# The experts layer computed by groups of four token tiles, with its weights held stationary

## The reference, cut to what matters

```python
shared = _silu_and_mul(x @ shared_gate_up_w.T) @ shared_down_w.T
shared = shared * jax.nn.sigmoid(x @ sgate_w.T)
routing_weights = jax.nn.softmax(x @ gate_w.T, axis=-1)
topk_w, topk_ids = jax.lax.top_k(routing_weights, 4)
for e in range(16):
    coef = jnp.sum(jnp.where(topk_ids == e, topk_w, 0.0), axis=-1)
    acc = acc + (_silu_and_mul(x @ w13[e].T) @ w2[e].T) * coef[:, None]
out = x_before_layernorm + shared + acc
```

## Time and profile before

| what | value |
|---|---|
| median of 3 runs | 3290.54 us (3288.26 to 3293.41) |
| the profiled execution's own time | 3290.39 us |
| its span in the trace | 3288.6 us |
| busy: PE, PEld, DVE, ACT, POOL | 2855.3, 1788.7, 1566.7, 1267.7, 1233.2 us |
| mean granted clock of PE, as a share of 2.4 GHz | 0.937 |
| experts stage, from its first instruction to the end of the span | 2635.61 to 3288.6 us |

### The profile page before, as it was taken

How to read it: one execution, slowest core, us unless ns; L and a number is a source line. 1 busy time by engine, 2 the same in 40 slices (tenths; PEclk the granted TensorE clock), 3 DMA queues, 4 the chain that set the end, 5 groups by cost and what they waited for, 6 DMA issues and landing times. The chain is left out here.

```text
span 3288.6 us, 50135 instructions
## 1 busy us (share of the span) xinstructions
PE 2855.3 (87%) x17687; PEld 1788.7 (54%) x17688; DVE 1566.7 (48%) x2714; ACT 1267.7 (39%) x2578; POOL 1233.2 (37%) x656
## 2 busy tenths in 40 slices
PE   6868444689999999999999999999978899999998
PEld 4646312554555555455545554555435567777776
DVE  3546587255445445544554455446427733333332
ACT  3437222134334433443344334334434423333332
POOL 0001000246567656765676576657650000000000
PEclk9879766779999999999999999999989999999999
DMA  1000300101111110110110111011012000000000
GB/s 42 0 15 0 125 0 0 59 26 41 37 40 36 40 36 25 51 40 25 36 51 33 33 36 51 25 40 36 31 39 115 1 1 0 0 0 0 0 0 26
DMA packets 26586, 98.13 MB, mean 30 GB/s; under 512 B 3808, under 2 KB 8544, under 8 KB 25120
## 3 DMA queue, kind: packets, MB, share of 16 engines
q1 hardware_dynamic: 24864, 94.15, 8.6%
q10 hardware_dynamic: 1664, 3.18, 0.3%
HBM read 55.71 MB, written 2.10 MB: 18 GB/s over the span
## 5 line engine op out<-in xcount | busy, mean ns | idle before, releaser
L742 POOL TENSOR_TENSOR cx_acc<-cx_acc,cx_prob 128x1024 f32<-128x1024 f32 (+1 forms) x352 | 834.5, 2371 | 509.1 <-ACT cx_prob L1022 501.6
L1022 ACT ACTIVATE cx_prob<-cx_st 128x512 f32<-128x512 f32 (+1 forms) x832 | 476.9, 596 | 595.4 <-PE cx_st L871 575.9
L1119 DVE TENSOR_REDUCE cx_mhalf<-cx_mx 128x1 f32<-128x804 f32 x512 | 486.3, 988 | 219.0 <-PE cx_mx L847 218.7
L882 PE MATMUL cx_av<-cx_prob,cx_kv 128*64 128x512 f32 (+1 forms) x1664 | 455.6, 626 | 0.0
L870 PE MATMUL cx_st<-cx_q,cx_k 128*128 128x512 f32 (+1 forms) x832 | 369.0, 444 | 49.7 <-ACT cx_prob L1022 49.0
L1585 PE MATMUL moe_gu<-moe_wgu,moe_xnT 128*128 128x352 f32 x1280 | 398.8, 463 | 0.0
L847 PE MATMUL cx_mx<-cx_kp,cx_q 128*128 128x402 f32 x1024 | 305.8, 382 | 61.9 <-DVE cx_mhalf L1119 58.6
L871 PE MATMUL cx_st<-cx_q,cx_k 128*128 128x512 f32 (+1 forms) x832 | 332.2, 399 | 0.0
L847 PEld LDWEIGHTS cx_mx<-cx_kp,cx_q 128*128 128x128 f32 x1024 | 176.0, 195 | 247.9 <-DVE cx_mhalf L1119 184.2
L1585 PEld LDWEIGHTS moe_gu<-moe_wgu,moe_xnT 128*128 128x128 f32 x1280 | 242.2, 191 | 124.7 <-issue 7.2
L1100 DVE TENSOR_TENSOR cx_turn<-cx_mx,cx_tab 128x384 f32<-128x384 f32 x256 | 130.9, 552 | 358.2 <-PE cx_mx L804 358.2
(11 more groups left out here) (210 smaller groups left out, 3648.3 us busy)
## 6 DMA issues: line engine op xcount, KB each, us to landing
cx_k<-cx_kp SPq DMA_DIRECT2D x32, 804.0 KB, 3.9
cx_ctx<-in_cx_ctxN SPq DMA_DIRECT2D x32, 416.0 KB, 3.3
cx_ctxr<-in_cx_ctxrN SPq DMA_DIRECT2D x32, 416.0 KB, 3.9
cx_k<-cx_kp SPq DMA_DIRECT2D x32, 402.0 KB, 5.1
moe_wgu<-in_moe_wgu SPq DMA_DIRECT2D x5, 1408.0 KB, 14.0
moe_wd<-in_moe_wd SPq DMA_DIRECT2D x4, 896.0 KB, 23.8
x_all<-in_x SPq DMA_DIRECT2D x1, 2048.0 KB, 3.9
cx_wq<-in_cx_wq SPq DMA_DIRECT2D x1, 2048.0 KB, 11.8
```

What stands on the lines that cost most here:

```text
L742: pool.tensor_tensor(acc[rows, :, :], sofar, prob[slot(kt)][rows, :, :], ALU.add).then_inc(s_acc, 1)
L882: last = pe.matmul(av[DCX * p:DCX * p + DCX, :], kv[e][0:nk(kt), kt, :], prob[slot(kt)][0:nk(kt), p, :], start=(kt == 0), stop=(kt == NKT ...
L1022: act.activation(prob[slot(kt)][rows, p, :], st[p][rows, :], ACT.Exp).then_inc(s_exp, 1)
L1119: dve.tensor_reduce(mhalf[:, i // 2, i % 2:i % 2 + 1], mx[i % 2][:, :, 0:KQ], AX.XY, ALU.max)\
```

## The change

The layer takes a group of four tiles (512 tokens) at a time, four groups in all, without a loop. The 3520 inner units are laid out as 28 chunks of 128 (the last padded with zeros), `moe_wgu` as `[P, 28, 2, DC, P]`. A chunk's weights are stationary and the 512 tokens of `xnT` move, so gate and up come out with inner units on partitions, ready for the down product: `turn` and its copies go. The coefficient is no longer one number per partition; a token's 17 coefficients (16 experts and the shared gate) are split in three bf16 parts (51 numbers), turned once per group by PE, and for each chunk a product with a 0/1 matrix `ownerb` of 51 rows spreads them to a PSUM tile `share` of 128 x 512. DVE multiplies silu with `share`, then with `up`. Each group is stored by its own DMA of 512 KB. The 0/1 matrix is one more load (f32, 51 x 3584) ahead of `a2`.

```diff
-    wgu = sb("moe_wgu", [P, NE, DC, 2 * FE])
+    wgu = sb("moe_wgu", [P, NFC, 2, DC, P])
+    owner = sb("moe_owner", [PARTS * CE, NFC, P])
-    pairs += [(wgu[:, 4 * i:4 * i + 4], a["moe_wgu"][:, 4 * i:4 * i + 4]) for i in range(NE // 4)]
+    pairs += [(wgu[:, 4 * i:4 * i + 4], a["moe_wgu"][:, 4 * i:4 * i + 4]) for i in range(NFC // 4)]
+    pairs += [(owner[:, :, :], a["moe_owner"])]
...
+    GATHER_AT = (3, 4)
+    NORM_AT = (6, 7)
+    TURN_AT = (9, 11)
+    KEEP_AT = (10, 12)
+    ROUTER_AT = 14
+    LOGITS_AT = 14
+    EXP_AT = 15
+    RANK_AT = 16
+    SPLIT_AT = 18
+    SPREAD_AT = 21
+    SPREAD_KEPT_AT = 22
...
+        @block.sync
+        def _(sp):
+            for g in range(NG):
+                sp.wait_ge(s_x, (g + 1) * GT)
+                sp.dma_start(out[g * GW:(g + 1) * GW, :].rearrange("(t p) d -> p t d", p=P),
+                             x_all[:, g * GT:(g + 1) * GT, :]).then_inc(s_out, 16)
...
+            def turn_coefficients(g):
+                pe.wait_ge(s_cf, g + 1)
+                for i in range(GT):
+                    last = pe.matmul(front[0:PARTS * CE, i * P:(i + 1) * P], parts[:, i, :, :], identb[:, :],
+                                     start=True, stop=True)
+            def gate_product(g, k):
+                if n >= 2:
+                    pe.wait_ge(s_silu, n - 1)
+                for c in range(DC):
+                    last = pe.matmul(gate[n % 2][:, :], wgu[:, k, 0, c, :], xnT[g % 2][:, c, :],
+                                     start=(c == 0), stop=(c == DC - 1))
+            def share_product(g, k):
+                if n == 0:
+                    pe.wait_ge(s_own, 1)
+                else:
+                    pe.wait_ge(s_gated, n)
+                pe.matmul(share[:, :], ownerb[:, k, :], coefT[g % 2][:, :], start=True, stop=True).then_inc(s_share, 1)
...
+            def down_product(g, k):
+                pe.wait_ge(s_hid, n + 1)
+                for i in range(GT):
+                    last = pe.matmul(acc[:, i, :], hidT[n % RING][:, i * P:(i + 1) * P], wd[:, k, :],
+                                     start=(k == 0 and i % 2 == 0), stop=(k == NFC - 1), skip_group_check=True)
...
+            turn_x(0, 0)
+            turn_x(0, 1)
+            router(0)
+            for g in range(NG):
+                for k in range(NFC):
+                    gate_product(g, k)
+                    if g == 0 and k == 0:
+                        up_product(g, k)
+                        turn_coefficients(0)
+                        share_product(g, k)
+                    else:
+                        share_product(g, k)
+                        up_product(g, k)
+                    if k >= LAG:
+                        down_product(g, k - LAG)
+                    elif g > 0:
+                        down_product(g - 1, NFC - LAG + k)
...
+            gather(0, 0)
+            gather(0, 1)
             normalise(0, 0)
-            logits(0, 0)
-            coefficients(0, 0)
-            rounds(dve, tile)
+            normalise(0, 1)
+            dve.tensor_copy(ownerb[:, :, :], owner[:, :, :]).then_inc(s_own, 1)
+            logits(0)
+            ranks(0)
+            split(0)
+            for g in range(NG):
+                for k in range(NFC):
+                    gated_product(g, k)
+                    hidden(g, k)
+                    if g > 0 and k == LAG - 1:
+                        update_x(g - 1)
...
-                sp.dma_start(out.rearrange("(t p) d -> p t d", p=P), x_all[:, :, :]).then_inc(s_out, 16)
```

More of the change, by code:

```diff
@@ new lines, in experts_weights, with experts_mlp @@
+    pairs += [(owner[:, :, :], a["moe_owner"])]
+    return (wgu, wd, wr, before, owner), pairs
+def experts_mlp(nc, sb, pb, sem, x_all, const, out, wgu, wd, wr, before, owner):
+    ident, identb = const["ident"], const["identb"]
+    stats = sb("moe_stats", [P, GT, 6])
+    mv = sb("moe_mv", [P, GT, 3])
+    rstd = sb("moe_rstd", [P, GT])
+    xn = sb("moe_xn", [P, GT, D])
+    xnT = [sb(f"moe_xnT{i}", [P, DC, GW]) for i in range(2)]
+    logit = sb("moe_logit", [P, GT, CE])
+    nmax = sb("moe_nmax", [P, GT])
+    rw = sb("moe_rw", [P, GT, CE])
+    rsum = sb("moe_rsum", [P, GT])
+    ahead = sb("moe_ahead", [P, GT, E, E])
+    equal = sb("moe_equal", [P, GT, E, E])
+    rank = sb("moe_rank", [P, GT, E])
+    coef = sb("moe_coef", [P, GT, CE])
+    rest = sb("moe_rest", [P, GT, CE])
+    parts = sb("moe_parts", [P, GT, PARTS, CE], BF16)
+    coefT = [sb(f"moe_coefT{i}", [PARTS * CE, GW], BF16) for i in range(2)]
+    ownerb = sb("moe_ownerb", [PARTS * CE, NFC, P], BF16)
+    RING = 3
+    silu = [sb(f"moe_silu{i}", [P, GW]) for i in range(RING)]
+    gated = [sb(f"moe_gated{i}", [P, GW]) for i in range(2)]
+    hidT = [sb(f"moe_hidT{i}", [P, GW]) for i in range(RING)]
+    gate = [pb(f"moe_gate{i}", [P, GW]) for i in range(2)]
+    up = [pb(f"moe_up{i}", [P, GW]) for i in range(2)]
+    share = pb("moe_share", [P, GW])
+    front = pb("moe_front", [P, GW])
+    acc = pb("moe_acc", [P, GT, D])
@@ L1531, in experts_mlp @@
     s_x = sem("moe_x_updated")
+    s_out = sem("moe_stored")
     s_dve = sem("moe_dve_step")
[L1533 to L1542, removed]
-    with nc.Block() as block:
+    LAG = 2
+    LAST = NG - 1
+    GATHER_AT = (3, 4)
+    NORM_AT = (6, 7)
+    TURN_AT = (9, 11)
+    KEEP_AT = (10, 12)
@@ L1546, in _ @@
         @block.gpsimd
         def _(pool):
[L1548 to L1558, removed]
+            for g in range(NG):
+                for half in range(2):
+                    tiles = slice(2 * half, 2 * half + 2)
+                    pool.wait_ge(s_var, 2 * g + half + 1)
+                    pool.tensor_tensor(rstd[:, tiles], mv[:, tiles, 1],
+                                       const["minus_half"][:, 0:1].broadcast_to([P, 2]), ALU.pow).then_inc(s_rstd, 1)
@@ new lines, in router @@
+            def router(g):
+                pe.wait_ge(s_xTc, 2 * g + 2)
+                for i in range(GT):
+                    for c in range(DC):
+                        last = pe.matmul(front[:, i * CE:(i + 1) * CE], xnT[g % 2][:, c, i * P:(i + 1) * P],
+                                         wr[:, c, :], start=(c == 0), stop=(c == DC - 1))
+                last.then_inc(s_rl, 1)
+            def turn_coefficients(g):
[3 more added lines that the diff above has]
+                                     start=True, stop=True)
+                last.then_inc(s_cT, 1)
@@ L1572, in router, with up_product @@
+            def up_product(g, k):
+                n = chunk(g, k)
+                if n >= 2:
+                    pe.wait_ge(s_hid, n - 1)
                 for c in range(DC):
-                    last = pe.matmul(front[:, 0:E + 1], xnT[g][:, c, :], wr[:, c, :],
+                    last = pe.matmul(up[n % 2][:, :], wgu[:, k, 1, c, :], xnT[g % 2][:, c, :],
                                      start=(c == 0), stop=(c == DC - 1))
[L1575 to L1626, removed]
@@ L1628, in _ @@
-            turn_x(0, 0)
-            router(0, 0)
-            rounds(pe, tile)
+                last.then_inc(s_up, 1)
+            def down_product(g, k):
+                n = chunk(g, k)
+                pe.wait_ge(s_hid, n + 1)
+                if k == 0 and g > 0:
+                    pe.wait_ge(s_x, g * GT)
+                for i in range(GT):
+                    last = pe.matmul(acc[:, i, :], hidT[n % RING][:, i * P:(i + 1) * P], wd[:, k, :],
+                                     start=(k == 0 and i % 2 == 0), stop=(k == NFC - 1), skip_group_check=True)
+                last.then_inc(s_down, 1)
@@ L1632, in _ @@
+            for k in range(NFC - LAG, NFC):
+                down_product(LAST, k)
         @block.scalar
         def _(act):
[L1634 to L1668, removed]
-            keep_xT(0, 0)
-            router_exp(0, 0)
@@ L1672, in _, with keep_xT, router_exp @@
-            rounds(act, tile)
+            def keep_xT(g, half):
+                act.wait_ge(s_xT, 2 * g + half + 1)
+                if g > 1:
+                    act.wait_ge(s_up, chunk(g - 2, NFC))
+                for i in range(2):
+                    at = (2 * half + i) * P
+                    last = act.copy(xnT[g % 2][:, :, at:at + P],
+                                    front[:, i * D:(i + 1) * D].rearrange("p (c t) -> p c t", c=DC))
+                last.then_inc(s_xTc, 1)
+            def router_exp(g):
+                act.wait_ge(s_lg, g + 1)
+                for i in range(GT):
+                    act.activation(rw[:, i, 0:E], logit[:, i, 0:E], ACT.Exp, bias=nmax[:, i:i + 1],
+                                   accum_out=rsum[:, i:i + 1])
+                act.activation(rw[:, :, E:CE], logit[:, :, E:CE], ACT.Exp, scale=-1.0).then_inc(s_rx, 1)
@@ new lines, in keep_coefficients, with silus @@
+            def keep_coefficients(g):
+                act.wait_ge(s_cT, g + 1)
+                if g > 1:
+                    act.wait_ge(s_share, chunk(g - 2, NFC))
```

(52 more changed lines are left out.)

205 lines of the change are left out of this document (118 added, 87 removed).

## The result

The changed kernel takes 3312.91 us (median of 4 runs, 3309.15 to 3317.11) against 3289.74 us of the kernel before in the same session: ratio 1.0069, 95% interval 1.0052 to 1.0087, slower by some 23 us. The forecast was 3314. Its profiled execution took 3309.15 us, with a span of 3307.4.

What follows compares the result with a forecast made beforehand. The prediction took PE, with no idle time, to bound the kernel. It added +24.2 us to the last product, -2.3 at the end and +1.5 for loads, +23.4 on 3290.39: 3314 us, range 3295 to 3328.

Steps and rivals of the forecast that it cites:

- The shape changes: On PE between gate, share and up: 51 rows run as 64, costing 0.30 us a chunk, 34 us in all.
- rival C: At share: bf16 load in the smaller shape slow and exposed like an f32 one, +10 us, 3324; chance 0.14.
- Columns: PE's gate, up, down and spreading products per chunk: 5.38 us, times 112 chunks 603 us.
- The fronts: PE's transposes, router and coefficients' turn for the next group: three of 3.2 us, 9.5 us.
- The start: First norm to last product: 668.6 us against 644.4, with a 7.0 us PE wait and 3.3 lost to the clock.
- The end: After the last product: adds and a 512 KB store of 4.1 us, 6.3 us in all, -2.3.
- The loads: SP's issues ahead of a2: three more of 0.51 us, on the path, +1.5 us (bound 0).
- my +22: The experts stage: +24.2 us up to the last product and -2.3 us at the end.

Runs made afterwards that it cites:

- e1: Changed kernel with the spreading product's contraction at 68 rows in place of 51 (a fourth, zero part): 3279.48 us, ratio to the kernel before 0.9973.
- e7: Changed kernel with three extra f32 products, result overwritten, between the first up product and the coefficients' turn: 3311.42 us.
- e10: Changed kernel with moe_wgu loaded in four pieces of 1.8 MB in place of seven of 1 MB: 3309.42 us.
- e6: Kernel before with its last inner piece padded from 64 to 128 rows (zeros): 3282.13 us, ratio to the kernel before 0.9981.
- e2: Changed kernel with the spreading product of 51 rows issued twice in a row in each chunk: 3338.33 us.
- e8: Changed kernel without the spreading products, gated being silu times silu: 3256.53 us.
- e4: Changed kernel with gate and up of chunk 1 issued ahead of the coefficients' turn, first group only: 3311.03 us.

## Why the prediction was right, by its steps

- **The shape changes**, 0.30 us a chunk and 34 us in all: measured 0.30 and, by e1, 33.4 us. That 51 rows step down to a smaller shape, taken from the 64-row and the one-column operands, was the step with the greatest weight: without it the forecast would have been 3279, and e1 gives 3279.5 (with the two opposite errors named below in it as well, so part of that closeness is luck). The rows behind this step were thin: they show that 64 rows and one column change the shape, and nothing on a size between two shapes. That the bf16 load is not exposed like an f32 one (rival C) shows in `share`, 0.39 us long against 0.38 in e1.
- **Columns**, 5.38 us a chunk from rows of 352, 256 and bf16 512: measured in e1. Nothing on DVE or ACT stopped PE. The fronts: 3.2 us each, and the distances between `share` products exceed 5.68 by 0.44, 0.44, 1.78 and 0.53 at the four places where they lie, 3.19.
- **The start** came out 2.3 us too long: 668.6 us expected to the last product, 666.3 measured. The first gate was right (10.4 for 10.7), the first `share` too (22.2 for 22.7), but not what lies between: the forecast had the clock rise 6.6 us after the router's start, as before, and it rose some 9.4 us after it (2643.20 to about 2652.6, by the 0.53 granted from 2646.64 to 2653.00), near the end of chunk 0's products. These took 6.5 us in place of 5.0, and so PE waited less, 4.6 us in place of 7.0. With the same code up to there the rise came some 6.2 us after the router's start in e7, so the rows fix no such distance. After the wait the half clock cost 2.3 us (e7) and not 3.3.
- **The end**: 4.8 us from the last product in place of 6.3; the 512 KB landed in 3.2 us and not 4.1, and nothing lies behind it.
- **The loads** were mis-sized: +1.5 expected for three issues of 0.5 us, +5.2 measured, since the last three took 1.4 to 2.1 us each; with three issues fewer none did (e10). The median's +23 is +18 from the stage and +5 from here; my +22 and +1.5 made the same sum by errors of opposite sign, 3.8 and 3.7 us. That the forecast met the median to 1 us is luck; that the stage has 34 us of shape changes in it is not.

The Trainium skill's page "TensorEngine Tiling (Array Packing)", Key Properties, by which a change of mode drains the engine, agrees with e1 and e6; these put its price at 0.09 us and the exposed load on top. The Trainium skill's page "TensorE: Matmul & The Clock Gate", Why this matters for your kernels, has a single product of 32 rows take the time of one of 128. No run here has 32 rows; one of 51 rows took its columns alone only behind another of 51 (e2, 0.22 us), and between full ones it cost 0.51 (e8).

## What to carry to other kernels

Count the changes of an operand's shape in PE's order as a cost of their own, 0.2 us each for f32 here, and look for them in the distances between starts, since PE's busy share hides them. An operand with fewer rows between full ones may be worth padding: here 51 rows paid and 68 did not, and a last piece of 64 rows was cheaper at 128. Sizes below 51 and between 64 and 68 were not tried. Fewer columns on a saturated engine are a gain only after this is paid. What SP issued ahead of its wait for the attention's weights was on the path, and the last of many issues took longer than the first; look at each issue's duration, and try fewer and larger ones.

## What the runs showed that I had not expected

- Fourteen DMA issues went through at 0.35 to 0.71 us each, and the fifteenth to seventeenth took 1.4 to 2.1; with four large pieces in place of seven, none took more than 0.64.
- PE's granted clock fell to 0.50 after three idle pieces of 0.47, 0.67 and 0.86 us, close together (e4), and stayed at 1.00 with idle times of 0.39 and 0.67 us (e7).
